# Layer-1 FFN down-projection: the first token tile's matmuls wait for one requantised block at a time, not for all 32

## The reference

```python
def act_quant(x):
    scale = 127.0 / jnp.clip(jnp.max(jnp.abs(x), axis=-1, keepdims=True), 1e-05)
    return jnp.clip(jnp.round(x * scale), -128, 127) / scale
def weight_quant(w):
    scale = 1.0 / jnp.clip(jnp.mean(jnp.abs(w)), 1e-05)
    return jnp.clip(jnp.round(w * scale), -1, 1) / scale
h = bit_linear(x, w1)                 # 1024 -> 4096
h = depthwise_conv1d(h.transpose(0, 2, 1), conv_w, conv_b).transpose(0, 2, 1)
h = jax.nn.silu(h)
return bit_linear(h, w2)              # 4096 -> 1024: the part that is changed
```

## Time and profile before

| | us |
|---|---|
| median of the runs shown (2) | 4879.96 |
| lowest, highest of these | 4855.28, 4904.65 |
| the profiled execution's own time | 4857.46 |
| its span, slowest core (core 2) | 4855.9 |
| spans of the other seven cores | 4817.4 to 4831.9 |
| TensorE busy in the span | 2584.6 (53%) |
| VectorE busy in the span | 1556.1 (32%) |
| mean granted TensorE clock, core 2 | 0.663 |

### The profile page before, as it was taken

The page is one execution under the profiler, slowest core; times in us unless marked ns, Lnnn a source line. Parts: engine busy times, 40 slices in busy tenths (PEclk is TensorE's granted clock), DMA queues, the critical chain, the costliest instruction groups (busy, mean ns, idle before and its releaser), DMA issues. The chain is left out here.

```text
span 4855.9 us, 46838 instructions; the slowest of 8 cores (4817.4 to 4855.9 us)
## 1 busy us (share of the span) xinstructions
PE 2584.6 (53%) x16028; PEld 1313.6 (27%) x16028; DVE 1556.1 (32%) x3161; ACT 864.2 (18%) x1405; POOL 291.1 (6%) x475
## 2 busy tenths in 40 slices
PE   1666787875499993665533333354016762024445
PEld 1324455544244441222222222232002221011112
DVE  4222211114211114111233333325665554543332
ACT  1003444541010101000033323312002221000000
POOL 0100000001220200010000000010000000100000
PEclk9875555557699996666655555566557776567777
DMA  3110000001671710010000000010340002521112
GB/s 82 14 18 1 1 1 1 1 6 14 82 74 15 76 15 8 12 13 11 9 1 1 1 1 1 1 14 5 62 78 39 39 39 56 74 48 35 35 35 87
DMA packets 186068, 134.33 MB, mean 28 GB/s; under 512 B 108016, under 2 KB 163312, under 8 KB 183792
## 3 DMA queue, kind: packets, MB, share of 16 engines
q0 software_dynamic: 147200, 97.70, 14.1%
q1 hardware_dynamic: 38640, 33.64, 2.3%
HBM read 187.02 MB, written 25.17 MB: 44 GB/s over the span
## 5 line engine op out<-in xcount | busy, mean ns | idle before, releaser
L561 PE MATMUL g1hp<-b4q1T,b4tern 128*128 128x512 bf16 x1024 | 300.0, 465 | 213.4 <-ACT b4hsp L579 124.5
L1567 PE MATMUL a0sb<-b1qTa,b1kTa 17*128 17x128 bf16 x2176 | 341.1, 301 | 1.7 <-PEq L1484 1.7
L1581 PE MATMUL a0yp<-b1vaug,b1Bp 128*128 128x65 bf16 x2176 | 225.2, 237 | 120.3 <-DVE b1Bp L1654 46.5
L1639 ACT ACTIVATE b1Bp<-a0sb 128x512 bf16<-128x512 f32 x384 | 229.2, 597 | 307.4 <-PE a0sb L1567 227.4
L1654 DVE TENSOR_TENSOR b1Bp<-b1Bp,b1tril 128x128 bf16<-128x128 bf16 x256 | 57.3, 225 | 542.4 <-ACT b1Bp L1634 540.7
L561 PEld LDWEIGHTS g1hp<-b4q1T,b4tern 128*128 128x128 bf16 x1024 | 114.8, 114 | 398.1 <-issue 327.5
L207 PE MATMUL f0gps<-b2lnT,b2wg 128*128 128x512 bf16 x768 | 177.8, 386 | 68.7 <-DMA b2wu<-f0wu 66.0
L1581 PEld LDWEIGHTS a0yp<-b1vaug,b1Bp 128*128 128x128 bf16 x2176 | 136.8, 117 | 255.8 <-issue 254.9
L1567 PEld LDWEIGHTS a0sb<-b1qTa,b1kTa 17*128 17x128 bf16 x2176 | 183.7, 124 | 38.9 <-issue 2.1
L1143 ACT ACT_TABLE_LOAD x32 | 41.1, 1283 | 773.5 <-PE a1a0g0sl L1073 577.8
L214 PE MATMUL f0ups<-b2lnT,b2wu 128*128 128x512 bf16 x768 | 173.6, 379 | 0.0
(11 more groups left out here) (793 smaller groups left out, 3979.0 us busy)
## 6 DMA issues: line engine op xcount, KB each, us to landing
b4big<-g1w POOLq DMA_DIRECT2D x16, 1024.0 KB, 9.6
hs_scr<-b4hsp POOLq DMA_DIRECT2D x32, 512.0 KB, 2.9
b4big<-g1w POOLq DMA_DIRECT2D x64, 256.0 KB, 4.2
b4big<-hs_scr SPq DMA_DIRECT2D x64, 256.0 KB, 4.7
b2wg<-f0wg POOLq DMA_DIRECT2D x48, 256.0 KB, 4.7
b2wu<-f0wu POOLq DMA_DIRECT2D x48, 256.0 KB, 5.3
xs<-x SPq DMA_DIRECT2D x1, 8192.0 KB, 29.9
xo<-xs SPq DMA_DIRECT2D x1, 8192.0 KB, 22.0
```

Of the source, the lines that this page charges most:

```text
L561: mm = t.matmul(hp[:, c % 2, n4 * 512:(n4 + 1) * 512], t1v[:, j, c * 128:(c + 1) * 128], q1T[:, j, n4 * 512:(n4 + 1) * 512], start=(j == 0 ...
L1567: t.matmul(sbat[:, gb % 2, jj * 128:(jj + 1) * 128], kT[hb:hb + 17, oc, j * 128:(j + 1) * 128], qT[hb:hb + 17, oc, i * 128:(i + 1) * 128], ...
L1581: mm = t.matmul(yps[:, h, 0:65], Bp[:, gb % 2, jj * 128:(jj + 1) * 128], v_aug[:, j, 65 * h:65 * h + 65], start=(k == 0 and jj == 0), stop ...
L1639: s.activation(Bp[:, gb % 2, 0:128 * nj], sbat[:, gb % 2, 0:128 * nj], AF.Square).then_inc(ph_s, 1)
```

## The change

Line 701 is taken out of the loop over token tiles and put into the loop over channel blocks, for tile 0 only. Instead of one wait for all 32 casts, block `c` waits for `c + 1` of them. For tile 1 no wait on `fc_s` is left: tile 0's last block has waited for all 32 on the same engine, ahead of it. Lines from 702 on move down by one; line 706 becomes 707, 731 becomes 732.

```diff
                 for tc in range(2):
-                    t.wait_ge(fc_s, Bc + NC_)
                     if tc >= 1:
                         t.wait_ge(fr_s, Br + tc)
                     for c in range(NC_):
+                        if tc == 0:
+                            t.wait_ge(fc_s, Bc + c + 1)
                         for n2 in range(2):
                             mm = t.matmul(dps[:, tc % 2, n2 * 512:(n2 + 1) * 512],
                                           hs_sb[:, c, tc * 128:(tc + 1) * 128],
```

## The result

| | before | after |
|---|---|---|
| median, us | 4896.54 (10 runs) | 4750.85 (11 runs) |
| lowest to highest | 4848.77 to 4955.87 | 4728.1 to 4832.04 |
| the profiled execution's own time | 4857.46 | 4738.32 |
| ratio after / before, 95% interval | | 0.9736 (0.968 to 0.9793) |

The change makes the kernel faster by 2.6% (2.1 to 3.2%). The medians and ranges of the table take in all executions; in three of the 11 after (4826.88 to 4832.04) cores of one die show a lower granted clock than the others and end later, so the ratio is taken without such executions, before and after (the others after have a median of 4738). The predicted 4736 lies 15 us under the median of the table and 2 us from the profiled execution; the range held. Between the profiled executions there are 119.1 us.

The account below looks back on a forecast made before the run. TensorE and VectorE were taken to bound the last stage by taking turns. The profiled 4857.5 us, less 123.8 of removed idle time, plus 2.0 for clock falls between tiles, gave 4735.7; range 4712 to 4795, the forecast's own 4715 to 4762.

Parts of the forecast that it names:

- The bound: Last stage: TensorE and VectorE take turns; VectorE's mean idle 16.3 us before each piece's first add is nearly all removable.
- the seam: Between a piece's two tiles: clock may fall in TensorE's 1.5 us idle; one piece in seven, 2 us added.
- The remaining 0.86 us: Path left from a piece's last cast to its first residual add, holding one block only: 0.86 us.
- The added waits at 0: 31 more TensorE waits per piece, 248 in all, stay hidden and cost 0; other end 0.6 us.
- The slow start lies under the casts: TensorE's half-clock start, 1.7 us and more per piece, leaves the path; caught up by about block 12 of 32.
- The clock while VectorE sets the pace: First tile: clock rises after 3.4 to 6 us and stays at 1.00 despite TensorE's gaps; forecast's chance 0.80.
- A: Rival: TensorE's clock swings in the gaps while VectorE sets the pace; 22 us more, 4756; chance 0.10.
- B: Rival: clock stays low for the whole first tile; first add waits 5.7 us, total 4797; chance 0.04.
- D: Rival: VectorE is slowed by TensorE reading the same buffer; 10% would be 18 us, 4754; chance 0.03.
- C: Rival: clock stays low into the second tile too; 148 us over the sum, 4882, slower; chance 0.02.
- E: Rival: change does nothing because TensorE waits for something other than the cast; 4857; chance 0.01.

Follow-up runs that it names:

- g8: Changed kernel with tile 0 waiting only at every 8th block, for 8 casts at once; last stage 424.2 us mean, 28.0 over the changed kernel.
- g16: Changed kernel with tile 0 waiting for 16 casts at once, twice a tile; last stage 445.5 to 450.5 us on six cores, 49 to 54 over.
- dve2: Changed kernel with VectorE's multiplication done twice, step 1.2 us instead of 0.70; last stage 535.2 us mean, 139 over the changed kernel.
- nofr: Changed kernel without tile 1's wait for tile 0's residual add; last stage 379.5 us mean, 16.7 under the changed kernel.
- dma8: Changed kernel with a semaphore for each of a piece's 8 loads; last stage 350.3 us, 45.9 under the changed kernel.
- inter: Changed kernel with both token tiles summed block by block, no wait between them; median 4685.05 us, ratio 0.9644 to the kernel before.
- interdma: Both token tiles block by block, plus a semaphore for each of a piece's 8 loads; median 4638.63 us, ratio 0.9534 to the kernel before.

## Why the prediction was right

Point by point:

- **The bound.** Two engines that take turns, with 16.3 us of the turn removable: right. The stage is shorter by 123.7 us on core 2, where the clock never fell at the seam, and by 118.3 in the mean of all cores, whose idle time before was 2 us less than core 2's (128.7 against 130.7) and which pay 3.8 at the seam.
- **The remaining 0.86 us.** Measured 0.84 or 0.85 in all 64 pieces. g8 and g16 show that the same sum holds with 8 and 16 blocks in it.
- **The added waits at 0.** Right: they add nothing to the 0.84, and the pairs of weight loads follow each other at 0.70 us.
- **The slow start lies under the casts.** Right: 3.4 us at 0.50 after 4468.8, and VectorE's step is reached before 4475, earlier than the 12 blocks that the prediction allowed. Over all 64 pieces the clock rose 2.8 to 6.0 us after the first matmul.
- **The clock while VectorE sets the pace (forecast against A and B).** Right: 1.00. Rival A would have made 4756 of the time. The Trainium skill (TensorE: Matmul & The Clock Gate, "A second HAM failure mode: psum-queue depth-cycling") tells of a kernel in which short idle spells between groups of matmuls come often enough to make the clock swing; the trace after does not show that for a step of 0.70 us (1.00), dve2 does for one of 1.2 us (0.63).
- **The seam.** The mechanism was right, the size was not: I took one piece in seven, 2 us, and it was 18 in 64, 3.8 us (5.1 on core 0). nofr shows that the idle 1.5 us is needed for it, g8 and the kernel before that it is not enough by itself.
- **VectorE unharmed (D).** Right: 418 and 294 ns as before.
- **C and E.** Nothing of either is seen.
- **The range.** Its upper end for the forecast, 4762, does not follow from its own terms: 4736 and 22 us are 4758. No reading depends on it.

The forecast sum was 4735.7 for the execution profiled; the one profiled after took 4738.32. That the two lie so close is in part luck. The stage alone gives 120.6 us from core 2 before (516.8) to the mean of the cores after, and 119.3 to core 0 after (397.5). The start of the stage on the slowest core was almost the same in the two profiled executions (4316.6 and 4316.8), and it need not have been.

## What to carry to other kernels

Where a semaphore is counted up once per block and nothing else holds the consumer, the consumer can wait for it once per block as well. What it gives is read from two rows: the consumer's time per block against the producer's, and the number of blocks that are left after the last release. Where TensorE becomes the one that waits, look at the granted clock there and at the seams: a pause of 1.5 to 2 us in or after stretches with gaps cost up to 1.7 us more in a seventh to a half of the pieces (9 of 64 in g16, 13 in dma8, 18 in the changed kernel, 34 in g8). A seam goes away together with a wait that was never needed (the other half of a PSUM tile), and the same reading (what does each wait of the piece wait for?) then found 46 us in the wait for all 8 loads.

## What the runs showed of the hardware that I had not expected

**A granted clock of 0.81.** In some executions pairs of cores (0 and 1, 2 and 3, 4 and 5, 6 and 7) had stretches at 0.81, both cores of a pair at nearly the same times, while others had 1.00. Two windows of inter, first core 4, then core 2, both dense:

```profile
4316.00:4334.00 18.00, 17.91 (x69) 7.46 (x69) 7.13 (x23) 0.00 (x0) 0.00 (x0) 0.81 0.00 0
```

```profile
4324.00:4338.00 14.00, 13.95 (x65) 6.37 (x65) 7.20 (x23) 0.00 (x0) 0.00 (x0) 1.00 0.00 1
```

69 matmuls in 18 us are 0.26 us each, 65 in 14 are 0.215. In the last stage only cores 4 and 5 had it in this run, and the same two in g16, where a second tile of core 4 took 16.96 us. The stages of cores 4 and 5 in inter are 353.6 and 354.3 us, about 18 more than the others'. In g8, g16, dve2 and inter it also occurs ahead of the last stage, on some cores and for up to 369 us in all, which bears on their whole times and not on the stages compared here. The profiled executions before and after, and those of nofr, dma8 and interdma, have none of it. Dense work on all cores did not bring it about by itself: in the kernel before each of the 8 cores has two stretches of 256 us in layer-0 FFN with TensorE 96 to 97% busy, at 1.00 throughout. What sets it off was not tried.

**Where the spread of the whole time comes from.** The start of the last stage differs by up to 39 us from core to core in the kernel before. Most of it arises in the projections of layer-1 attention (lines 910 and 960), where TensorE works in short bursts between loads. The same stretch of the same program on two cores before, core 1 and then core 2:

```profile
1885.50:2381.60 496.10, 275.50 (x908) 103.46 (x908) 76.83 (x58) 2.37 (x3) 49.62 (x94) 0.75 0.11 13
```

```profile
1889.80:2421.70 531.90, 310.96 (x912) 112.54 (x912) 76.84 (x58) 2.37 (x3) 49.63 (x94) 0.67 0.10 12
```

With a mean clock of 0.75 it takes 496 us, with 0.67 it takes 532: the clock swings in both, in another rhythm. 36 us are nearly a third of what this change gives, so for a change of this size the stage has to be read by itself.
